# Bucket bits with bits on partitions, and values straight into two padded buffers, in a one-core attention and feed-forward kernel

## The chip, the cores and the metric

The kernel runs on one core of a Trainium2 chip. The metric is the device time of one execution in microseconds (us). Engines are called as in the profile: PE (matrix engine), PEld (its weight loads), DVE (vector), ACT (scalar), POOL (GpSimd) and SP (the queue that issues all DMAs here).

## What is computed

The input x has 16 batches of 512 tokens with 128 features. Each batch goes through hashed attention (16 heads of 8 features) and a feed-forward part; both are layer-normed and added to the residual. What matters for the change is the bucket of each token and head, and the values:

```python
q = (x @ Wq.T + bq).reshape(B, S, H, Dh)
v = (x @ Wv.T + bv).reshape(B, S, H, Dh)
qa = concatenate([q, ones], axis=-1)
proj = einsum('bshe,en->bshn', qa, hyperplanes)          # 6 hyperplanes
bits = (proj >= 0).astype(int32)
buckets = einsum('bshn,n->bsh', bits, 2 ** arange(6))
same = (buckets of s == buckets of t)
attn = softmax(q q^T / sqrt(128) * (62 + same))          # per head
out = attn @ v
```

Afterwards `y1 = x + layernorm(out)`, and the feed-forward part takes the layer-normed y1 through a gated layer of 512 hidden features (Silu), two hidden layers 512 x 512 (Gelu) and an output layer, then the output is `y1 + layernorm(ffn)`.

## The kernel before

One batch is one iteration of `stages` (line 348), and several batches are under way at once: in iteration i the kernel attends to batch i, projects batch i+1 (buckets and values), makes the queries of batch i+2, and runs the feed-forward of batches i-1 and i-2. Iterations -2, -1 and 0 start this up; iterations 2 to 14 carry everything up to the projection, iteration 14 makes no more queries, iteration 15 does not project.

An iteration has 64 slots (`TILES`), one for each score tile of 128 x 512 (16 heads times 4 row tiles). Every engine runs through the same slots in its own program; what it does in a slot is fixed by the constants of lines 55 to 133 (`PROJ_SLOT`, `V_SLOT` and so on), and inside a slot by the order in `iteration`. There is no dynamic order: an engine that waits for a semaphore holds up all that stands behind it. The steady work of a slot is:

- PE: the score tile (line 496) into one of four banks; every fourth slot the row maxima of a head are spread (line 504). The score of tile k waits until DVE has finished tile k-3.
- DVE: the coefficients 62 + same (line 695) for tile k+1, then coefficient times score and its row maximum (line 714); seven heads have one subtraction of the maximum on DVE (line 830).
- ACT copies maxima (line 942); POOL subtracts scores from them (line 899); ACT takes exponentials of two tiles (line 951).
- PE weighs the values with the probabilities, four heads at a time (line 525), in slots 27, 29 and 30 of each quad of heads (`PV_LAGS`), into the one auxiliary bank `aux_bank`. Projections, values, rows and queries use that bank too, in turns.

The steps around the change, by slot, in iterations from 2 on:

- Slot 18: ACT copies the values `v_next` of the batch now attended into `v_pad` (line 1063), where each head has 32 columns: 8 values, a one, zeros.
- Slot 19: PE projects the queries on the hyperplanes, four matmuls of 96 columns (line 568), tokens on partitions; DVE adds the bias in PSUM (line 779).
- Slot 20: DVE compares with zero and multiplies with powers of two (line 785).
- Slot 21: DVE sums the six bits (line 792) into `bcol`, read by the coefficients of the next iteration as a column per head and row tile.
- Slot 21 also holds, on ACT, two Gelus of the second hidden layer (line 1037, `SECOND_GELU_SLOTS` 85 = 64 + 21) and then the normalisation of the attention result (line 956); POOL adds the residual in slot 22 (line 917), DVE takes the statistics of it in slot 23 (line 722).
- Slot 24: PE makes the values (line 557), which wait for the bits since both use `aux_bank`; DVE adds the bias into `v_next` (line 774); ACT casts `bcol` to bf16 (line 994).
- Slot 27: the first weighing (line 525) waits for the value add, `pe.wait_ge(v_next_done, b + 2)` in line 515, since it overwrites that bank.
- Slot 36: PE turns the bucket columns into rows with an identity (line 579), ACT copies them (lines 1002, 1004), SP stores and later broadcasts them.
- Slots 77 to 94, that is 13 to 30 of the next iteration, hold the second hidden layer on PE (line 639), slots 57 to 72 the first (line 629).

At the very start DVE fills `pow2_sb` and clears the stacks, POOL makes an identity and clears `v_pad` (lines 870 to 877), and DVE casts the identity to bf16 (line 837) before its first statistics.

Of the kernel before, what the change touches and what calls it, by code (L numbers as in the profile page):

```python
# [102 lines left out]
V_PAD_SLOT = 18  # L103
# [33 lines left out]
def sandwich_kernel(nc, x, wqT, bq, wvT, bv, hyper_blocks, hyper_bias, w1T, w2T, h1T, h2T, scales, w3T, w3_s, out):  # L137
    ctx = ExitStack()
    with ctx:  # L139
# [19 lines left out]
        hbias_sb = sb("hbias_sb", [P, NH, H])  # L159
        pow2_sb = sb("pow2_sb", [P, NH, H])  # L160
# [8 lines left out]
        ident16 = sb("ident16", [P, P], BF16)  # L169
# [13 lines left out]
        v_next = sb("v_next", [P, ST, H, DH])  # L183
        proj = sb("proj", [P, ST, NH, H])
        bcol16 = sb("bcol16", [P, ST, H], BF16)
# [12 lines left out]
        v_pad = sb("v_pad", [P, ST, H, VW])  # L198
# [48 lines left out]
        v_next_done = sem("v_next_done")  # L247
        proj_psum = sem("proj_psum")
        proj_done = sem("proj_done")
        bits_done = sem("bits_done")  # L250
        bcol_done = sem("bcol_done")
        bcol16_done = sem("bcol16_done")
# [6 lines left out]
        v_pad_done = sem("v_pad_done")  # L259
# [104 lines left out]
        def _(sp):  # L364
            sp.dma_start(x_in[:], x_view[0]).then_inc(x_loaded, 16)
            for dst, src in (
                (wq_sb[:], wqT), (bq_sb[:], bq.rearrange("(p a) -> p a", a=1)),
                (wv_sb[:], wvT), (bv_sb[:], bv.rearrange("(a e) -> a e", a=1).broadcast_to([P, E])),
                (hyper_sb[:], hyper_blocks),
                (hbias_sb[:].rearrange("p n h -> p (n h)"),  # L370
                 hyper_bias.rearrange("(a e) -> a e", a=1).broadcast_to([P, NH * H])),
            ):
                sp.dma_start(dst, src).then_inc(projection_in, 16)
# [93 lines left out]
        def _(pe):  # L467
            pe.wait_ge(projection_in, 16 * PROJECTION_DMAS)
            pe.wait_ge(consts_made, 4)
# [38 lines left out]
            def weigh_values(b, quad, j, query, project):  # L508

                if j == 0:  # L510
                    if quad == 0:
                        pe.wait_ge(v_pad_done, b + 1)

                    if quad == 0 and project:
                        pe.wait_ge(v_next_done, b + 2)
# [8 lines left out]
                for hh in range(4):  # L524
                    last = nc.tensor.matmul(aux_bank[hh * VW:(hh + 1) * VW, :], v_pad[:, j, quad * 4 + hh, :],  # L525
                                            probs[:, quad % 2, hh, j, :], start=(j == 0), stop=(j == ST - 1))
# [25 lines left out]
            def project_step(p, k, attend):  # L552
                if k == V_SLOT:
                    if begun(p):
                        pe.wait_ge(bits_done, p + 1)
                    for t in range(ST):
                        last = nc.tensor.matmul(projection_bank(p, 1)[:, t * P:(t + 1) * P], xnT[:, t * P:(t + 1) * P], wv_sb[:],
                                                start=True, stop=True)
                    last.then_inc(v_psum, 1)
                if k == PROJ_SLOT:  # L560
# [4 lines left out]
                    if begun(p - 1):  # L565
                        pe.wait_ge(att_done, (p - 1) * QUADS)
                    for t in range(ST):
                        last = nc.tensor.matmul(projection_bank(p, 0)[:, t * NH * H:(t + 1) * NH * H], qT[:, t * P:(t + 1) * P],
                                                hyper_sb[:], start=True, stop=True)
                    last.then_inc(proj_psum, 1)  # L570
                if k == ROW_SLOT:
                    pe.wait_ge(consts_made, 5)
                    pe.wait_ge(bcol16_done, p + 1)
# [3 lines left out]
                    for t in range(ST):  # L577

                        last = nc.tensor.matmul(projection_bank(p, 2)[0:H, t * P:(t + 1) * P], bcol16[:, t, :], ident16[:],
                                                start=True, stop=True)  # L580
                    last.then_inc(brow_psum, 1)
# [102 lines left out]
        def _(dve):  # L684
            for n in range(NH):
                last = nc.vector.memset(pow2_sb[:, n, :], float(2 ** n))
            last.then_inc(consts_made, 1)
# [77 lines left out]
            def project_step(p, k):  # L765
                if k == V_ADD_SLOT:
                    dve.wait_ge(v_psum, p + 1)
                    if begun(p):

                        dve.wait_ge(v_pad_done, p)  # L770
                    if isinstance(p, int) and p == 0:

                        dve.wait_ge(projection_in, 16 * PROJECTION_DMAS)
                    nc.vector.tensor_tensor(v_next[:].rearrange("p t h d -> p t (h d)"),
                                            projection_bank(p, 1)[:].rearrange("p (t e) -> p t e", t=ST),
                                            bv_sb[:].unsqueeze(1).broadcast_to([P, ST, E]), ALU.add).then_inc(v_next_done, 1)
                if k == PROJ_ADD_SLOT:
                    dve.wait_ge(proj_psum, p + 1)
                    nc.vector.tensor_tensor(projection_bank(p, 0)[:, 0:ST * NH * H].rearrange("p (t e) -> p t e", t=ST),
                                            projection_bank(p, 0)[:, 0:ST * NH * H].rearrange("p (t e) -> p t e", t=ST),  # L780
                                            hbias_sb[:].rearrange("p n h -> p (n h)").unsqueeze(1).broadcast_to([P, ST, NH * H]),
                                            ALU.add).then_inc(proj_done, 1)
                if k == BITS_SLOT:
                    dve.wait_ge(proj_done, p + 1)
                    nc.vector.scalar_tensor_tensor(out=proj[:].rearrange("p t n h -> p t (n h)"),
                                                   in0=projection_bank(p, 0)[:, 0:ST * NH * H].rearrange("p (t e) -> p t e", t=ST),
                                                   scalar=0.0,
                                                   in1=pow2_sb[:].rearrange("p n h -> p (n h)").unsqueeze(1).broadcast_to([P, ST, NH * H]),
                                                   op0=ALU.is_ge, op1=ALU.mult).then_inc(bits_done, 1)
                if k == BUCKET_SLOT:  # L790
                    dve.wait_ge(bits_done, p + 1)
                    nc.vector.reduce_sum(bcol[:, p % 2], proj[:].rearrange("p t n h -> p t h n"), AXIS_X).then_inc(bcol_done, 1)
# [76 lines left out]
        def _(pool):  # L869
# [4 lines left out]
            nc.gpsimd.memset(v_pad[:, :, :, DH:DH + 1], 1.0).then_inc(v_pad_clear, 1)  # L874
# [3 lines left out]
            pool.wait_ge(consts_made, 4)  # L878
# [55 lines left out]
        def _(act):  # L934

            act.wait_ge(consts_made, 4)
# [103 lines left out]
            def iteration(i, query, project, attend, feed, finish):  # L1040
# [3 lines left out]
                for k in range(TILES):  # L1044
# [12 lines left out]
                    if k == V_PAD_SLOT and attend:  # L1057
                        act.wait_ge(v_next_done, i + 1)

                        if begun(i):  # L1060
                            act.wait_ge(pv_psum, i * QUADS)
# [48 lines left out]
```

## Time and profile before

| | before |
|---|---|
| median of 3 runs | 1501.82 us (1500.60 to 1503.36) |
| profiled execution, its own time | 1501.84 us |
| its span in the profile | 1499.6 us |
| mean granted clock of PE | 0.985 of full |
| instructions | 22142 |

A group's row gives the engine, the operation, what it writes and reads with shapes, how often it ran, its busy time, the mean of one, and the idle time of the engine just before it with what ended it. A timeline row gives the start and the length in us; neighbours of one kind are merged into a row with their count. An idle time in brackets stands in front of the instruction. PE's rows end later than the next one starts, since matmuls are pipelined: how long PE is held is read from start to start. A few matmul records are missing from the trace.

### The profile page before, as it was taken

What the parts mean: (1) busy time and instruction counts of PE and PEld (TensorE: products, weight loads), DVE (VectorE), ACT (ScalarE), POOL (GpSimd) and SP (SyncE); (2) the same over time, 40 slices, a digit from 0 to 9 for tenths busy, and PEclk for the clock granted to TensorE, in tenths of its full rate; (3) what the DMA queues carried; (4) which work ended last, traced back from release to release, by engine and by line L of the source; (5) the groups of instructions that cost most, each with busy time, mean ns of one, the idle gap of its engine ahead of it and who ended that gap; (6) DMA issues with size and microseconds to landing.
All of it is one profiled execution on the core that took longest, in us unless ns stands there. A gap on an engine that the chain in (4) does not pass through costs nothing. (4 is left out here: it accounts for less than half of the span.)

```text
span 1499.6 us, 22142 instructions
## 1 busy us (share of the span) xinstructions
PE 1349.9 (90%) x6502; PEld 625.1 (42%) x6624; DVE 1310.9 (87%) x4026; ACT 1182.8 (79%) x1603; POOL 1216.0 (81%) x809
## 2 busy tenths in 40 slices
PE   3677899999999999999999999899999989999996
PEld 2222344353444435344443534444353444434343
DVE  4999999999999999999999999999999999998620
ACT  2565888888788888878888887888888798888831
POOL 1898979888979988897998889799888979888810
PEclk9888999999999999999999999999999999999999
DMA  5422232222223222222322222232222223212000
GB/s 137 128 55 68 69 85 63 68 68 66 58 68 93 60 71 68 62 62 68 93 58 73 68 60 64 69 93 55 76 69 58 66 68 86 56 50 68 8 1 14
DMA packets 62793, 100.00 MB, mean 67 GB/s; under 512 B 7888, under 2 KB 43984, under 8 KB 62672
## 3 DMA queue, kind: packets, MB, share of 16 engines
q1 hardware_dynamic: 62672, 98.58, 23.6%
q8 instruction: 53, 0.87, 0.3%
q14 instruction: 68, 0.56, 0.1%
HBM read 83.60 MB, written 14.95 MB: 66 GB/s over the span
## 5 line engine op out<-in xcount | busy, mean ns | idle before, releaser
L899 POOL TENSOR_TENSOR logits<-max_row,logits 128x1024 f32<-128x1024 f32 (+1 forms) x512 | 1075.2, 2131 | 133.1 <-ACT max_row L942 130.5
L714 DVE CUSTOM_DVE_ANT_0 logits<-s_bank,coeff 128x512 f32<-128x512 f32 x1024 | 698.4, 683 | 0.6 <-issue 0.6
L695 DVE TENSOR_SCALAR coeff<-brow,bcol 128x516 bf16<-128x516 bf16 x1024 | 483.1, 472 | 79.9 <-PE s_bank L496 37.9
L951 ACT ACTIVATE probs<-logits 128x1024 f32<-128x1024 f32 x512 | 525.5, 1054 | 7.4 <-POOL logits L899 5.1
L496 PE MATMUL s_bank<-mov_stack,stat_stack 128*128 128x512 bf16 x902 | 319.2, 389 | 87.5 <-DVE rowmax L714 43.5
L496 PEld LDWEIGHTS s_bank<-mov_stack,stat_stack 128*128 128x128 bf16 x1024 | 95.2, 98 | 431.2 <-issue 212.0
L525 PE MATMUL aux_bank<-probs,v_pad 128*32 128x512 f32 x2048 | 263.6, 610 | 7.7 <-issue 4.1
L942 ACT COPY max_row<-s_bank 128x512 f32<-128x512 f32 x256 | 148.5, 580 | 137.9 <-PE s_bank L504 136.6
L629 PE MATMUL f_bank<-hid_a,h_sb 128*128 128x512 f32 x512 | 243.1, 596 | 14.9 <-DVE hid_a L809 12.9
L639 PE MATMUL f_bank<-hid_b,h_sb 128*128 128x512 f32 x512 | 249.3, 600 | 1.6 <-ACT hid_b L1032 1.4
L504 PE MATMUL s_bank<-ident,rowmax 128*128 128x128 f32 x1024 | 157.2, 277 | 7.7 <-issue 2.5
L504 PEld LDWEIGHTS s_bank<-ident,rowmax 128*128 128x128 f32 x1024 | 127.4, 139 | 63.9 <-DVE rowmax L714 25.9
L629 PEld LDWEIGHTS f_bank<-hid_a,h_sb 128*128 128x128 f32 x512 | 91.5, 190 | 88.8 <-issue 64.0
L639 PEld LDWEIGHTS f_bank<-hid_b,h_sb 128*128 128x128 f32 x512 | 88.4, 190 | 85.1 <-issue 80.8
L951 ACT ACT_TABLE_LOAD x87 | 111.6, 1283 | 1.5
L525 PEld LDWEIGHTS aux_bank<-probs,v_pad 128*32 128x32 f32 x2048 | 47.8, 109 | 104.0 <-issue 96.9
L714 DVE DVE_READ_ACCUMULATOR2_ANT rowmax<- 128x1 f32 x1024 | 87.3, 85 | 0.0
L830 DVE TENSOR_TENSOR logits<-s_bank,logits 128x512 f32<-128x512 f32 x112 | 77.1, 688 | 3.9 <-ACT max_row L942 3.9
L883 POOL TENSOR_SCALAR end_shift<-end_mv 128x4 f32<-128x4 f32 x16 | 3.1, 193 | 85.3 <-DVE end_mv L727 85.3
L956 ACT ACTIVATE ffn<-ffn,end_bias,end_rstd 128x128 f32<-128x128 f32 x64 | 26.4, 482 | 57.7 <-POOL end_bias L888 57.7
L604 PE MATMUL f_bank<-ynT,w_sb 128*128 128x512 f32 x128 | 66.8, 606 | 1.1 <-ACT ynT L1022 0.7
L618 PE MATMUL f_bank<-ynT,w_sb 128*128 128x512 f32 x128 | 67.0, 606 | 0.3 <-DVE rowmax L714 0.3
(95 smaller groups left out, 1197.1 us busy)
## 6 DMA issues: line engine op xcount, KB each, us to landing
brow<-bucket_scratch SPq DMA_DIRECT2D x64, 522.0 KB
mov_stack<-q_scratch SPq DMA_DIRECT2D x192, 96.0 KB
stat_stack<-q_scratch SPq DMA_DIRECT2D x192, 96.0 KB
q_scratch<-q_parts SPq DMA_DIRECT2D x16, 384.0 KB, 5.4
x_in<-in_x SPq DMA_DIRECT2D x16, 256.0 KB, 7.0
q_scratch<-q_parts SPq DMA_DIRECT2D x16, 256.0 KB, 6.8
x_res<-in_x SPq DMA_DIRECT2D x16, 256.0 KB, 2.9
out<-ffn SPq DMA_DIRECT2D x16, 256.0 KB, 2.6
```

Of the source, the lines that this page charges most:

```text
L496: nc.tensor.matmul(tile_bank(k)[:], stat_stack[:, quad % 2, hh, t * P:(t + 1) * P], mov_stack[:, quad % 2, hh, :], start=True, stop=True). ...
L504: last = nc.tensor.transpose(maxima_bank(h)[:, t * P:(t + 1) * P], rowmax[:, h * ST + t:h * ST + t + 1].broadcast_to([P, P]), ident[:])
L525: last = nc.tensor.matmul(aux_bank[hh * VW:(hh + 1) * VW, :], v_pad[:, j, quad * 4 + hh, :], probs[:, quad % 2, hh, j, :], start=(j == 0), ...
L618: nc.tensor.matmul(f_bank[UP_BANKS[j]][:], w2_sb[:, col], ynT[:], start=True, stop=True).then_inc(w2_psum, 1)
L629: last = nc.tensor.matmul(f_bank[FIRST_HIDDEN_BANKS[j]][:], h1_sb[:, k, col], hid_a[:, k, :], start=(k == 0), stop=(k == HT - 1))
L639: last = nc.tensor.matmul(f_bank[SECOND_HIDDEN_BANKS[j]][:], h2_sb[:, k, col], hid_b[:, k, :], start=(k == 0), stop=(k == HT - 1))
L695: nc.vector.tensor_scalar(coeff[:, k % 3, :].rearrange("p (r n) -> p r n", r=ROW_RUNS), brow[:, h // 4 % 2, h % 4, :, 0:RUN], bcol[:, b % ...
L714: nc.vector.tensor_tensor_reduce(out=logits[:, k % RING, :], in0=tile_bank(k)[:], in1=coeff[:, k % 3, 0:SEQ], scale=float(E) ** -0.5, scal ...
L830: nc.vector.tensor_tensor(logits[:, k % RING, :], maxima_bank(h)[:], logits[:, k % RING, :], ALU.subtract).then_inc(shared_below_max_done, 1)
L899: nc.gpsimd.tensor_tensor(tiles, max_row[:, h % 2, :].unsqueeze(1).broadcast_to([P, n, SEQ]), tiles, ALU.subtract).then_inc(below_max_done, 1)
L942: nc.scalar.copy(max_row[:, h % 2, :], maxima_bank(h)[:]).then_inc(max_row_done, 1)
L951: nc.scalar.activation(probs[:, h // 4 % 2, h % 4, t:t + 2, :], logits[:, k % RING:k % RING + 2, :], ACT.Exp, scale=-1.0).then_inc(probs_d ...
```

## The change

The projection is turned: `hyper_sb` (96 columns) is the stationary operand and all 512 tokens are streamed, so that the 96 bits (6 hyperplanes x 16 heads) lie on partitions. One DVE operation adds the bias, now a column, and compares, and writes bf16 bits. A matrix `weights` with 2^n at (bit n of head h, head h) makes buckets out of bits by matmul: four small ones at slot 21 with the bits stationary give columns, one of 512 columns at slot 36 with the weights stationary gives rows. ACT copies the columns from PSUM to `bcol` in slot 21. The value add moves to slot 25 and writes into one half of a doubled `v_pad`; the copy of slot 18, `v_next`, the bf16 identity and the cast are gone. POOL builds the weights at the start with six selects; DVE casts them before its first statistics. The program is also built with a smaller DMA scratch (8192).

```diff
-V_ADD_SLOT = 24
+V_ADD_SLOT = 25
-PROJ_ADD_SLOT = 19
 BITS_SLOT = 20
-BUCKET_SLOT = 21
-BUCKET_CAST_SLOT = 24
+BCOL_SLOT = 21
+BCOL_COPY_SLOT = 21
-V_PAD_SLOT = 18
...
-        v_pad = sb("v_pad", [P, ST, H, VW])
+        v_pad = sb("v_pad", [P, 2, ST, H, VW])
...
                     if quad == 0:
-                        pe.wait_ge(v_pad_done, b + 1)
+                        pe.wait_ge(v_added, b + 1)
                     if quad == 0 and project:
-                        pe.wait_ge(v_next_done, b + 2)
+                        pe.wait_ge(v_added, b + 2)
...
+                if k == PROJ_SLOT:
...
+                    nc.tensor.matmul(projection_bank(p, 0)[0:NH * H, :], hyper_sb[:], qT[:], start=True,
+                                     stop=True).then_inc(proj_psum, 1)
+                if k == BCOL_SLOT:
+                    pe.wait_ge(weights_made, 1)
+                    pe.wait_ge(bits_done, p + 1)
+                    for t in range(ST):
+                        last = nc.tensor.matmul(projection_bank(p, 0)[:, t * H:(t + 1) * H], bitsT[:, t * P:(t + 1) * P],
+                                                weights16[:], start=True, stop=True)
+                    last.then_inc(bcol_psum, 1)
                 if k == V_SLOT:
                     if begun(p):
-                        pe.wait_ge(bits_done, p + 1)
+                        pe.wait_ge(bcol_done, p + 1)
...
-                        last = nc.tensor.matmul(projection_bank(p, 2)[0:H, t * P:(t + 1) * P], bcol16[:, t, :], ident16[:],
-                                                start=True, stop=True)
-                    last.then_inc(brow_psum, 1)
+                    nc.tensor.matmul(projection_bank(p, 2)[0:H, :], weights16[:], bitsT[:], start=True,
+                                     stop=True).then_inc(brow_psum, 1)
...
                 if k == V_ADD_SLOT:
                     dve.wait_ge(v_psum, p + 1)
...
+                    nc.vector.tensor_tensor(v_pad[:, p % 2, :, :, 0:DH],
+                                            projection_bank(p, 1)[:].rearrange("p (t h d) -> p t h d", t=ST, d=DH),
+                                            bv_sb[:].rearrange("p (h d) -> p h d", d=DH).unsqueeze(1).broadcast_to([P, ST, H, DH]),
+                                            ALU.add).then_inc(v_added, 1)
+                if k == BITS_SLOT:
+                    dve.wait_ge(proj_psum, p + 1)
...
+                    nc.vector.tensor_scalar(bitsT[:], projection_bank(p, 0)[0:NH * H, :], hbias_sb[:], 0.0, ALU.add,
+                                            ALU.is_ge).then_inc(bits_done, 1)
...
-                    dve.wait_ge(consts_made, 4)
-                    nc.vector.tensor_copy(ident16[:], ident[:]).then_inc(consts_made, 1)
+                    dve.wait_ge(weights_built, NH + 1)
+                    nc.vector.tensor_copy(weights16[:], weights_sb[:]).then_inc(weights_made, 1)
...
+            nc.gpsimd.memset(weights_sb[:], 0.0).then_inc(weights_built, 1)
+            for n in range(NH):
+                pool.wait_ge(weights_built, n + 1)
+                nc.gpsimd.affine_select(out=weights_sb[:], in_=weights_sb[:], compare_op=ALU.not_equal,
+                                        fill=float(2 ** n), base=-H * n, pattern=[[-1, H]],
+                                        channel_multiplier=1).then_inc(weights_built, 1)
...
-                if k == BUCKET_CAST_SLOT:
-                    act.wait_ge(bcol_done, p + 1)
-                    nc.scalar.copy(bcol16[:], bcol[:, p % 2]).then_inc(bcol16_done, 1)
+                if k == BCOL_COPY_SLOT:
+                    act.wait_ge(bcol_psum, p + 1)
+                    if p > 1:
+                        act.wait_ge(coeff_done, (p - 1) * TILES)
+                    nc.scalar.copy(bcol[:, p % 2],
+                                   projection_bank(p, 0)[:, 0:ST * H].rearrange("p (t h) -> p t h", t=ST)).then_inc(bcol_done, 1)
...
-                    if k == V_PAD_SLOT and attend:
-                        act.wait_ge(v_next_done, i + 1)
...
-                        nc.scalar.copy(v_pad[:, :, :, 0:DH], v_next[:]).then_inc(v_pad_done, 1)
...
-    nc = bacc.Bacc("TRN2", target_bir_lowering=False, num_devices=1)
+    nc = bacc.Bacc("TRN2", target_bir_lowering=False, num_devices=1, dynamic_dma_scratch_size=8192)
```

## Rows read from the trace of the kernel before

**Rows 1.** The page, part 1: busy time, share of the span, instructions by engine.
```profile
PE 1349.9 (90%) x6502; PEld 625.1 (42%) x6624; DVE 1310.9 (87%) x4026; ACT 1182.8 (79%) x1603; POOL 1216.0 (81%) x809
```

**Rows 2.** Groups by line, whole span: busy us, mean ns | idle before.
```profile
L792 DVE TENSOR_REDUCE bcol<-proj 128x64 f32<-128x384 f32 x16 | 13.0, 814 | 0.0
...
L1063 ACT COPY v_pad<-v_next 128x512 f32<-128x512 f32 x16 | 10.0, 622 | 0.0
...
L779 DVE TENSOR_TENSOR aux_bank<-aux_bank,hbias_sb 128x384 f32<-128x384 f32 x15 | 8.5, 564 | 0.0
L785 DVE SCALAR_TENSOR_TENSOR proj<-aux_bank,pow_sb 128x384 f32<-128x384 f32 x15 | 8.3, 555 | 0.0
...
L994 ACT CAST bcol<-bcol 128x64 bf16<-128x64 f32 x16 | 3.7, 230 | 4.0 <-DVE bcol L792 4.0
```

**Rows 3.** Waits of DVE, 600 to 1290 us (eight iterations): total, times, longest.
```profile
DVE coeff L695 <- PE s_bank L496: 18.6, 32, 1.2
DVE coeff L695 <- remote: 16.1, 8, 2.0
```

**Rows 4.** Timeline, slots 18 to 27: start us, us, engine, line [idle before <-releaser].
```profile
741.35 1.03 PE L568 MATMUL aux_bank<-hyper_sb,qT 128*128 128x96 f32 x8
...
742.21 1.05 PE L639 MATMUL f_bank<-hid_b,h_sb 128*128 128x512 f32 x2
...
743.10 0.38 PE L496 MATMUL s_bank<-mov_stack,stat_stack 128*128 128x512 bf16 x1
...
743.50 1.28 ACT L1037 ACT_TABLE_LOAD   x1
743.51 0.48 DVE L695 TENSOR_SCALAR coeff<-brow,bcol 128x516 bf16<-128x516 bf16 x1
...
744.52 0.56 DVE L785 SCALAR_TENSOR_TENSOR proj<-aux_bank,pow_sb 128x384 f32<-128x384 f32 x1
...
745.03 0.38 PE L496 MATMUL s_bank<-mov_stack,stat_stack 128*128 128x512 bf16 x1
...
745.23 1.27 ACT L1037 ACTIVATE hid_a<-f_bank,scales_sb 128x512 f32<-128x512 f32 x2 [0.45 <-PE f_bank L639]
...
745.45 0.48 DVE L695 TENSOR_SCALAR coeff<-brow,bcol 128x516 bf16<-128x516 bf16 x1 [0.37 <-PE s_bank L496]
...
748.11 1.27 POOL L917 TENSOR_TENSOR y<-y,x_res 128x512 f32<-128x512 f32 x1 [0.34 <-ACT y L956]
...
749.41 0.88 DVE L722 BATCH_NORM_STATS2 att_stats<-y 128x6 f32<-128x128 f32 x4
...
751.19 0.69 DVE L774 TENSOR_TENSOR v_next<-aux_bank,bv_sb 128x512 f32<-128x512 f32 x1
...
753.56 1.92 PE L525 MATMUL aux_bank<-probs,v_pad 128*32 128x512 f32 x16
```

**Rows 5.** Timeline, six iterations later, slot 21.
```profile
1271.00 0.48 DVE L695 TENSOR_SCALAR coeff<-brow,bcol 128x516 bf16<-128x516 bf16 x1 [0.38 <-PE s_bank L496]
```

**Rows 6.** Timeline, the end of slot 30 and slot 31.
```profile
758.70 1.98 PE L639 MATMUL f_bank<-hid_b,h_sb 128*128 128x512 f32 x4
...
760.94 0.48 DVE L695 TENSOR_SCALAR coeff<-brow,bcol 128x516 bf16<-128x516 bf16 x1 [2.01 <-remote]
```

**Rows 7.** Timeline of ACT, slot 52.
```profile
785.66 0.59 ACT L976 COPY xnT<-aux_bank 128x512 f32<-128x512 f32 x1 [0.41 <-PE aux_bank L546]
786.26 1.28 ACT L1027 ACT_TABLE_LOAD   x1
```

**Rows 8.** Timeline, the first 21 us.
```profile
0.90 1.80 POOL L872 MEMSET v_pad<- 128x2048 f32 x1
...
5.57 0.85 DVE L722 BATCH_NORM_STATS2 x_stats<-x_in 128x6 f32<-128x128 f32 x4
...
17.19 1.97 PE L557 MATMUL f_bank<-wv_sb,xnT 128*128 128x128 f32 x8
...
20.35 0.58 PE L579 MATMUL f_bank<-ident,bcol 128*16 128x128 bf16 x4 [1.19 <-ACT bcol L994]
```

More of the change, by code:

```diff
@@ L524, in weigh_values @@
                 for hh in range(4):
-                    last = nc.tensor.matmul(aux_bank[hh * VW:(hh + 1) * VW, :], v_pad[:, j, quad * 4 + hh, :],
+                    last = nc.tensor.matmul(aux_bank[hh * VW:(hh + 1) * VW, :], v_pad[:, b % 2, j, quad * 4 + hh, :],
                                             probs[:, quad % 2, hh, j, :], start=(j == 0), stop=(j == ST - 1))
@@ L552, in project_step @@
             def project_step(p, k, attend):
-                if k == V_SLOT:
-                    if begun(p):
-                        pe.wait_ge(bits_done, p + 1)
-                    for t in range(ST):
-                        last = nc.tensor.matmul(projection_bank(p, 1)[:, t * P:(t + 1) * P], xnT[:, t * P:(t + 1) * P], wv_sb[:],
-                                                start=True, stop=True)
-                    last.then_inc(v_psum, 1)
                 if k == PROJ_SLOT:
@@ L566, in project_step @@
                         pe.wait_ge(att_done, (p - 1) * QUADS)
-                    for t in range(ST):
-                        last = nc.tensor.matmul(projection_bank(p, 0)[:, t * NH * H:(t + 1) * NH * H], qT[:, t * P:(t + 1) * P],
-                                                hyper_sb[:], start=True, stop=True)
-                    last.then_inc(proj_psum, 1)
+                    nc.tensor.matmul(projection_bank(p, 0)[0:NH * H, :], hyper_sb[:], qT[:], start=True,
[3 more added lines that the diff above has]
+                    pe.wait_ge(bits_done, p + 1)
+                    for t in range(ST):
+                        last = nc.tensor.matmul(projection_bank(p, 0)[:, t * H:(t + 1) * H], bitsT[:, t * P:(t + 1) * P],
+                                                weights16[:], start=True, stop=True)
+                    last.then_inc(bcol_psum, 1)
+                if k == V_SLOT:
+                    if begun(p):
+                        pe.wait_ge(bcol_done, p + 1)
+                    for t in range(ST):
+                        last = nc.tensor.matmul(projection_bank(p, 1)[:, t * P:(t + 1) * P], xnT[:, t * P:(t + 1) * P], wv_sb[:],
+                                                start=True, stop=True)
+                    last.then_inc(v_psum, 1)
                 if k == ROW_SLOT:
-                    pe.wait_ge(consts_made, 5)
-                    pe.wait_ge(bcol16_done, p + 1)
                     if attend:
                         pe.wait_ge(att_done, (p - 1) * QUADS + 1)
-                    for t in range(ST):
-                        last = nc.tensor.matmul(projection_bank(p, 2)[0:H, t * P:(t + 1) * P], bcol16[:, t, :], ident16[:],
-                                                start=True, stop=True)
-                    last.then_inc(brow_psum, 1)
+                    nc.tensor.matmul(projection_bank(p, 2)[0:H, :], weights16[:], bitsT[:], start=True,
+                                     stop=True).then_inc(brow_psum, 1)
             def ffn_step(f, slot, finish):
@@ L684, in _ @@
         def _(dve):
-            for n in range(NH):
-                last = nc.vector.memset(pow2_sb[:, n, :], float(2 ** n))
-            last.then_inc(consts_made, 1)
             nc.vector.memset(brow16[:], 0.0).then_inc(stacks_clear, 1)
@@ L767, in project_step @@
                     dve.wait_ge(v_psum, p + 1)
-                    if begun(p):
[L770 to L789, printed above, removed]
@@ L873, in _ @@
             pool.wait_ge(v_pad_clear, 1)
-            nc.gpsimd.memset(v_pad[:, :, :, DH:DH + 1], 1.0).then_inc(v_pad_clear, 1)
+            nc.gpsimd.memset(v_pad[:, :, :, :, DH:DH + 1], 1.0).then_inc(v_pad_clear, 1)
             pool.wait_ge(consts_made, 1)
```

39 lines of the change are left out of this document (18 added, 21 removed).

## The prediction

> **What bounds the kernel now.** I read the page first, then the groups by line, the waits, and the timeline of one iteration engine by engine. The page calls PE and DVE the two busiest engines [rows 1]; an average cannot say which of them a saving must come from, and the change takes work from DVE above all. The timeline can: the same event of two iterations six apart stands at 745.45 and 1271.00 us [rows 4, 5], so one iteration takes 525.55 / 6 = 87.59 us, and its pattern repeats to a hundredth. One iteration has 64 slots, a score tile each (about 1.0 us on DVE). In slots 0 to 31 PE also carries the hidden layers of the feed-forward: between 730 and 761 us no matmul row shows idle time in front of it, and it is DVE that waits. In eight iterations DVE waited 18.6 us for score matmuls and 16.1 us for "remote" [rows 3]. The second is PE too: DVE stands 2.01 us before slot 31's tile, until 760.94 [rows 6], just as PE is through with the four instructions that began at 758.70; that tile's matmul record is missing. So each iteration has 2.0 us of DVE waiting at slot 31, and the edited steps (slots 18 to 25) all lie in front of it. After slot 31 the roles change, but nothing of weight is edited there.
>
> **What the change removes from DVE.** Three operations of 0.564, 0.555 and 0.814 us [rows 2] go. By starts in the timeline they hold DVE 0.47, 0.47 and 0.73 us, 1.67 together. The new bits operation (96 x 512 out of PSUM) is not in the trace. Its lower bound is the 384-element comparison, 0.555; its upper one the 512-element add, 0.69 [rows 4]. The length is 512, so 0.69, which holds DVE 0.60. Net 1.07 us an iteration. None of it reaches the end in a full iteration: tile 20 starts at 743.51 because its score matmul began at 743.10 and took 0.38, and tile 21 at 745.45 for the one that began at 745.03 [rows 4]. The add before tile 20 becomes a wait, the comparison is replaced at its place, and the saved reduction comes before tile 22, where PE is next late and from where slot 31's wait swallows the rest.
>
> **What it does on PE.** The four projections (eight instructions from 741.35 until the next line starts at 742.21, 0.86 us) become one pair of 512 columns; the pair of that size at 742.21 is over when the score matmul starts at 743.10, 0.89 [rows 4]. Zero. The buckets' four small matmuls at slot 21 are new. Eight load-and-multiply steps of the projection take 0.86, 0.107 each, so four take 0.43; below, 0.1 (their 16 columns alone), above, 0.6 (loads not hidden). I take 0.43 by the nearest row. The row matmul at slot 36 gets shorter by at most 0.2 where PE waits for DVE: zero.
>
> **What it moves on ACT.** The 0.622 us copy into the padded buffer goes and the 0.230 us cast too [rows 2]; ACT has idle time there: zero. But the new copy of the bucket columns stands at slot 21 and waits for the new matmuls, and queued behind it on ACT are the load of the Gelu table, two Gelus, and the normalisation whose result DVE needs at slot 23. Now the table load runs at 743.50, before the Gelus are due, and they start at 745.23 when PE is ready [rows 4]. With the copy in front the load should come later: at slot 52 a copy that waits for PE stands ahead of a Silu, and the load began at 786.26, after the copy of 785.66 to 786.25 [rows 7]. Step by step: bits start at 744.52 (where the comparison starts now) and end at 745.21; the matmuls run from 745.26, and the last result is there at about 745.78; ACT sees it at 745.84; a copy of 0.23 ends at 746.07; the load of 1.28 ends at 747.36. The Gelus start at 747.37, 2.14 late. Normalisation and the residual on POOL (748.11 now) follow without slack, for DVE waits for them already: its statistics start at 749.41, 0.03 after POOL is done [rows 4]. They move to 751.55.
>
> **Who waits for that.** The value add moves from slot 24 to 25. After the statistics come tile 24 (start to start 1.78 with them), the moments 0.28, tile 25 0.99 and the add 0.69: it ends at 755.29. PE's value matmuls of slot 27 wait for this add because both use the auxiliary bank. They start at 753.56 now [rows 4], with 1.7 us in hand since the add started at 751.19. They would start at 755.34, 1.78 late. The four bucket matmuls' 0.43 lies inside that. PE has no idle time from there to slot 31, so that tile and the iteration are 1.78 us later. In the half after it DVE, PE, ACT and POOL are shifted alike; POOL's lost 2.1 us go into its idle time.
> This holds for the 13 iterations that carry projection, Gelu at slot 21 and residual together (2 to 14): 13 x 1.78 = 23.1 us.
>
> The load is 1.28 us in the trace, and the next activation starts right after it (743.50 to 744.78; the Gelus then wait for PE) [rows 4]. The Trainium skill, page "ScalarE: Activation LUTs", section "What ACT_TABLE_LOAD costs", gives 1283 ns for the load and about 1380 ns more for a drain, 2.66 us for each switch. By that the Gelus would start 1.38 us later still, and the 13 iterations would cost 18 us more.
>
> **First iterations and start.** In iterations 0 and 1 PE is light and DVE sets the pace; between 0 and 2 x 1.07 us are won, I take 1.1, since PE must now answer between slots 20 and 22. At the start POOL's clearing of the padded buffer doubles, 1.80 us more [rows 8], with the identity behind it. Then a small memset and six dependent selects of small size, not in the trace; POOL's small dependent steps are 0.27 apart, so 1.6 (bounds 0.1 and 0.4 each: 0.6 and 2.4). They are ready at about 6.9, DVE copies them, and the first statistics start at 7.1 instead of 5.57 [rows 8]: 1.5. Before the first bucket row PE now does the columns and the value product (1.97 [rows 8]) behind the bits: bits end at 18.64, columns 19.3, values 21.2, row 21.85, against 20.93 now (20.35 + 0.58): 0.9. The DMA issues follow the row. Start: 2.4 us, bounds 0.5 to 4.
>
> **Sum.** 23.1 + 2.4 - 1.1 = 24.4. The profiled execution took 1501.84 us (span 1499.6), the median is 1501.82, so no correction: 1526 us, 1.6% slower. A difference under 0.2% (3 us) is what a measurement of this kernel cannot tell from none.
>
> **Rivals.**
> A. The table load runs ahead of the copy, or the copy finds its data earlier. For: the load itself needs nothing of the copy. Against: rows 7. Then the Gelus start at 746.08, 0.85 late, the value add ends at 754.0 and PE is only 0.4 to 0.5 later an iteration: 13 x 0.45 + 1.3 = 7 us, 1509.
> B. Faster, because DVE's saving counts in full: the mechanism is that PE is not the last to arrive in slots 19 to 31, for example if it runs ahead as soon as DVE reads its banks sooner. Price 15 x 1.07 = 16.1, less 2.4 at the start: 1488. For: DVE's busy share [rows 1]. Against: the 2.01 us of waiting behind all the edits [rows 6]. It decides only where that wait would be under 1.07.
> C. Slower still, by the switch of 2.66 us, or with PE's later matmuls also running into DVE's shared subtraction at slot 27: 1544. Against: the trace's load has no such tail.
> D. As A, but with bucket matmuls of 0.1 and Gelus that PE keeps waiting anyway: 13 x 0.1 + 1.3 = 2.6 us, 1504, within what can be told from none.
>
> **Chances.** Forecast 0.62, A 0.18, B 0.08, C 0.07, D 0.05. The forecast's own range: the delay of 2.14 may be 0.4 smaller or larger (bucket matmuls 0.1 to 0.6, copy from PSUM 0.2 to 0.3), 13 x 0.4 = 5, and the start 2: 1519 to 1532. To hold the time 8 times in 10 the range reaches down through A: 1506 to 1532. Slower 0.62 + 0.18 + 0.07 = 0.87, same 0.05, faster 0.08.
>
> **What would show it.** Right: the period is about 89.4 us; the Gelu table load of slot 21 starts after the bucket copy, near 2.6 us later against slot 20 than now; DVE waits about 2 us for the residual before the statistics of slot 23; the value matmuls of slot 27 have about 1.4 us idle before them, released by the value add; slot 31's wait is still between 1.5 and 2 us. Wrong: a period under 88.1 (then A, or a smaller delay), a load that begins before the copy, a wait at slot 31 that is gone together with a period under 87 (B). If DVE shows no wait for the residual at slot 23, the step that fails is the one on ACT's queue.

## The result, and the profile after

The changed kernel takes 1526.23 us (median of 4 runs, 1524.69 to 1527.95) against 1501.59 us for the kernel before on the same chip: ratio 1.0163, 95% interval 1.0145 to 1.0181, so slower by 24.6 us. The forecast was 1526.0. The span of the profiled execution is 1524.2 us against 1499.6.

The page, part 1, of the changed kernel:

```profile
PE 1360.0 (89%) x6429; PEld 615.2 (40%) x6544; DVE 1296.2 (85%) x3988; ACT 1174.3 (77%) x1587; POOL 1218.9 (80%) x816
```

DVE's busy time fell by 14.7 us against [rows 1] and the span grew by 24.6: the saving is there and worth nothing. The new operations, groups by line (busy us, mean ns | idle before, and what ended it):

```profile
L776 DVE TENSOR_SCALAR bitsT<-aux_bank,hbias_sb 96x512 bf16<-96x512 f32 x15 | 11.1, 742 | 0.0
...
L767 DVE TENSOR_TENSOR v_pad<-aux_bank,bv_sb 128x512 f32<-128x512 f32 x15 | 10.3, 686 | 0.0
...
L988 ACT COPY bcol<-aux_bank 128x64 f32<-128x64 f32 x15 | 3.2, 212 | 40.6 <-PE aux_bank L561 40.6
```

ACT stood 40.6 us in front of fifteen copies of 0.212 us; the cast it replaces had 4.0 us in front of sixteen [rows 2]. The waits of DVE from 600 to 1310 us, eight iterations (total, times, longest):

```profile
DVE coeff L687 <- PE s_bank L491: 26.5, 48, 1.9
DVE att_stats L714 <- POOL y L908: 15.3, 8, 1.9
DVE coeff L687 <- remote: 13.7, 15, 1.9
```

The second line is new: eight waits of 1.9 us for the residual, absent from [rows 3]. The timeline of one iteration, slots 21 to 27 and 31 (a time here less 13.28 us compares with [rows 4, 6]: the comparison began at 744.52, the bits begin at 757.80):

```profile
757.80 0.74 DVE L776 TENSOR_SCALAR bitsT<-aux_bank,hbias_sb 96x512 bf16<-96x512 f32 x1
...
758.31 0.38 PE L491 MATMUL s_bank<-mov_stack,stat_stack 128*128 128x512 bf16 x1
...
758.68 0.24 PE L561 MATMUL aux_bank<-weights,bitsT 96*128 96x16 bf16 x4
...
758.78 1.11 PE L634 MATMUL f_bank<-hid_b,h_sb 128*128 128x512 f32 x2
...
758.97 0.21 ACT L988 COPY bcol<-aux_bank 128x64 f32<-128x64 f32 x1 [2.70 <-PE aux_bank L561]
...
759.20 1.28 ACT L1032 ACT_TABLE_LOAD   x1
...
760.49 1.26 ACT L1032 ACTIVATE hid_a<-f_bank,scales_sb 128x512 f32<-128x512 f32 x2
...
763.36 1.27 POOL L908 TENSOR_TENSOR y<-y,x_res 128x512 f32<-128x512 f32 x1 [2.32 <-ACT y L947]
...
764.67 0.87 DVE L714 BATCH_NORM_STATS2 att_stats<-y 128x6 f32<-128x128 f32 x4 [1.92 <-POOL y L908]
...
767.71 0.69 DVE L767 TENSOR_TENSOR v_pad<-aux_bank,bv_sb 128x512 f32<-128x512 f32 x1
...
768.46 0.19 PEld L520 LDWEIGHTS aux_bank<-probs,v_pad 128*32 128x32 f32 x8 [1.79 <-DVE v_pad L767]
...
768.49 1.92 PE L520 MATMUL aux_bank<-probs,v_pad 128*32 128x512 f32 x16 [1.24 <-ACT probs L942]
...
775.87 0.48 DVE L687 TENSOR_SCALAR coeff<-brow,bcol 128x516 bf16<-128x516 bf16 x1 [1.89 <-remote]
```

Read from the top: ACT is idle for 2.70 us at a copy of 64 columns, the table load starts only behind it, the Gelus come 1.98 us later than before (760.49 - 13.28 = 747.21 against 745.23), the residual and with it the statistics again 1.98 (751.39 against 749.41), the value add ends at 768.40, and the value matmuls of slot 27 start at 755.21 against 753.56: 1.65 late. Six iterations later the bits begin at

```profile
1293.08 0.74 DVE L776 TENSOR_SCALAR bitsT<-aux_bank,hbias_sb 96x512 bf16<-96x512 f32 x1
```

so the period is (1293.08 - 757.80) / 6 = 89.21 us against 87.59: 1.62 more, over 13 iterations 21.1 of the 24.6 us. The start, from the same timeline at its beginning, answers to [rows 8]:

```profile
0.90 3.51 POOL L857 MEMSET v_pad<- 128x4096 f32 x1
...
5.35 1.89 POOL L867 TENSOR_SCALAR_AFFINE_SELECT weights_sb<-weights_sb 96x16 f32<-96x16 f32 x6
...
7.35 0.86 DVE L714 BATCH_NORM_STATS2 x_stats<-x_in 128x6 f32<-128x128 f32 x4
...
22.63 0.60 PE L575 MATMUL f_bank<-bitsT,weights 96*16 96x512 bf16 x1
```

Where each tile comes late shows where the iteration loses (start of the tile's logits within an iteration, against the same tile before):

```
tile      19    22    23    24    26    28    31 to the end
after      0  -0.35 +0.17 +1.94 +1.94 +1.75  +1.62
```

Two steps need explaining: +1.9 at the statistics, and that 1.62 of it is never made good.

### The profile page after: what moved, and what is told of

Read it like the earlier page. It is cut to its first block and busy times, and to the rows that moved or that the text cites. A ratio compares the mean times of both kernels' runs of the same rounds, so it can differ in the third digit from the quotient of the medians.

```text
span 1524.2 us, 21959 instructions
## 1 busy us (share of the span) xinstructions
PE 1360.0 (89%) x6429; PEld 615.2 (40%) x6544; DVE 1296.2 (85%) x3988; ACT 1174.3 (77%) x1587; POOL 1218.9 (80%) x816
## 5 line engine op out<-in xcount | busy, mean ns | idle before, releaser
L491 PE MATMUL s_bank<-mov_stack,stat_stack 128*128 128x512 bf16 x909 | 324.1, 391 | 75.6 <-DVE rowmax L706 34.1
```

The costliest lines, as they stand in the source:

```text
L491: nc.tensor.matmul(tile_bank(k)[:], stat_stack[:, quad % 2, hh, t * P:(t + 1) * P], mov_stack[:, quad % 2, hh, :], start=True, stop=True). ...
```

## The experiments

Eleven kernels ran. The theory (T): the bucket copy on ACT, queued before the table load, delays the residual; the value add is queued on DVE behind the residual's statistics; PE waits for the add, and PE has no idle time to make that good before slot 31. The rivals: the delay comes from more work on PE; the wait in slot 27 is for ACT's exponentials, as the PE row above names it; or the doubled buffer and the direct value path cost the time.

**1. The copy off ACT's queue.** The same copy on DVE, in its slot; all else is the change.

```
 on DVE, slot 21:
+  dve.wait_ge(bcol_psum, p + 1)
+  nc.vector.tensor_copy(bcol[:, p % 2], projection_bank(p, 0)[:, 0:ST * H]...)
 on ACT, slot 21:
-  act.wait_ge(bcol_psum, p + 1)
-  nc.scalar.copy(bcol[:, p % 2], projection_bank(p, 0)[:, 0:ST * H]...)
```

> The changed kernel with one step moved: the bucket columns are copied out of PSUM by DVE in slot 21 instead of by ACT. Theory (the copy on ACT's queue holds back the Gelu table load, and through the residual and the value add PE's slot 27): the Gelus start when PE is ready, the value add ends before PE wants it, and the period falls from 89.21 to 87.59 + 0.10 (the four bucket matmuls, 0.10 as measured) = 87.7 us. Total about 1501.6 + 2.4 (start) + 1.3 + 0 to 2 for iterations 0 and 1: 1505 to 1508. Rival 1 (the bucket matmuls and the turned projection on PE are the cost): the period stays at 89.2, 1526. Rival 2 (writing values with a stride of 32, or the doubled buffer, slows the work): period stays above 88.5.

Measured: 1511.96 us (4 runs, 1510.20 to 1512.79), ratio to before 1.0066 (1.0049 to 1.0083), period 88.07: 1.14 of the 1.62 us are gone, and 14.3 us of the 24.6, though the same copy is still made. Waits of DVE, eight iterations:

```profile
DVE coeff L687 <- PE s_bank L491: 28.9, 53, 1.9
DVE coeff L687 <- remote: 18.4, 20, 1.9
```

The waits for the residual have left the list. So most of the loss is the copy's place in ACT's queue; but the total missed the expected 1505 to 1508, and what is left over lies in two places. In slot 27 PE still waits for the add:

```profile
672.36 0.69 DVE L767 TENSOR_TENSOR v_pad<-aux_bank,bv_sb 128x512 f32<-128x512 f32 x1
...
673.12 0.19 PEld L520 LDWEIGHTS aux_bank<-probs,v_pad 128*32 128x32 f32 x8 [0.78 <-DVE v_pad L767]
```

and in slot 21 the small matmuls cost PE 0.31 us (there the next score matmul starts 4.39 us after tile 19, 4.09 before). Both were tried next.

**2. The add one slot earlier,** ahead of the statistics' tile, where it was before; the copy stays on ACT.

```
-V_ADD_SLOT = 25
+V_ADD_SLOT = 24
```

> The changed kernel with the value add back in slot 24. The trace names the exponentials as what PE's value matmuls of slot 27 wait for (10.0 us in eight iterations); the theory says it is the value add, which ends 0.05 us before them too. Theory: with the add one tile earlier PE is next held by the shared subtraction of slot 27, which is 1.98 us late with 1.2 in hand: the period is 87.59 + 0.85 = 88.4 us, and iteration 1 no longer loses 2.5 us. Rival (the exponentials hold PE): the period stays at 89.2.

Measured: 1513.78 us (2 runs, 1513.5 to 1514.06), ratio 1.0080 (1.006 to 1.010), period 88.46. DVE still stands before the statistics, as in the change,

```profile
DVE att_stats L714 <- POOL y L908: 15.4, 8, 1.9
```

so the residual is as late as in the change, and yet 0.75 us an iteration come back. That names what PE waited for in slot 27: the add. The exponentials stood where they were (the one that ends as PE starts in the change begins 12.1 us after tile 19's logits in both kernels), while PE's value matmuls of slot 27 came from 13.16 to 11.90, ahead of it; so the PE row names the exponentials wrongly and the weight-load row above it (1.79 <-DVE v_pad) names the add rightly. Iteration 1 went from 85.10 to 81.51 us, which matters below.

The 0.87 us a period that are left are more than the value matmuls are late now (11.90 against 11.53, 0.37). The late residual reaches PE by a second road, as the expectation said: DVE is late with its tiles and with the shared subtraction of slot 27, and two score matmuls wait for it.

```profile
673.67 0.39 PE L491 MATMUL s_bank<-mov_stack,stat_stack 128*128 128x512 bf16 x1 [0.29 <-DVE rowmax L706]
...
675.37 0.38 PE L491 MATMUL s_bank<-mov_stack,stat_stack 128*128 128x512 bf16 x1 [0.31 <-DVE logits L815]
```

**3. The value path alone,** on the kernel before: the add writes into the doubled padded buffer, the ACT copy goes, everything of the buckets stays.

```
-v_pad = sb("v_pad", [P, ST, H, VW])
+v_pad = sb("v_pad", [P, 2, ST, H, VW])
-nc.vector.tensor_tensor(v_next[:]..., projection_bank(p, 1)..., bv_sb..., ALU.add)
+nc.vector.tensor_tensor(v_pad[:, p % 2, :, :, 0:DH], projection_bank(p, 1)..., bv_sb..., ALU.add)
-nc.scalar.copy(v_pad[:, :, :, 0:DH], v_next[:])
```

(The DMA scratch is cut to 8192 bytes, as in the change.)

> The kernel before with one part of the change alone: values are added straight into two padded buffers in slot 24 and the ACT copy of slot 18 is gone; projection, bits and buckets as before. Theory: the period stays at 87.59 us (ACT has idle time there) and only the longer clearing of the buffer shows at the start, if the identity is late for DVE's cast: at most 1.8 us, total 1501.6 to 1503.4. Rival: the freed 0.62 us of ACT is worth something, period under 87.4, or the strided add is slower and the period is above 87.8.

Measured: 1501.61 us (8 runs), ratio 1.0002 (0.9991 to 1.0012), period 87.59, to a hundredth that of before. The 0.622 us copy taken off ACT [rows 2] is worth nothing, and the direct path costs nothing. The period's whole loss belongs to the buckets and the slot of the add.

**4. The copy stays on ACT, one slot later,** behind the table load and the Gelus.

```
-BCOL_COPY_SLOT = 21
+BCOL_COPY_SLOT = 22
```

> The changed kernel with the copy still on ACT but in slot 22, behind the table load, the Gelus, the normalisation and the copy of the maxima. Theory: the residual chain is on time again, but PE's value matmuls of slot 24 wait for the copy, which ends 0.6 us after PE gets there: the period is 88.0 to 88.3 us. Rival (ACT's copy as such costs, wherever it stands): the period stays near 89.2.

Measured: 1515.35 us (2 runs), ratio 1.0091 (1.007 to 1.0111), period 88.44, a little above the 88.0 to 88.3 expected; the rival's 89.2 is out. No wait for the residual is left here either. So it was the place in ACT's queue, not the copy's being on ACT. The 0.37 above the copy on DVE is the link that the expectation named: PE's value matmuls of slot 24 need the bank of the columns and wait for the copy.

```profile
669.97 0.97 PEld L568 LDWEIGHTS aux_bank<-wv_sb,xnT 128*128 128x128 f32 x8 [0.59 <-ACT bcol L988]
```

The hidden-layer matmuls behind them start 0.36 us later than in experiment 1 (7.59 against 7.23 us after tile 19's logits).

**5. Experiments 1 and 2 together.**

> The changed kernel with the bucket columns copied by DVE in slot 21 and the value add in slot 24. With the copy alone moved the period was 88.07 us, 0.48 over before: PE was 0.31 late after the bucket matmuls, and its slot 27 stood 0.16 more for the value add in slot 25. Theory: with both edits only PE's 0.31 is left, period 87.9 us, and iterations 0 and 1 gain about 1 us each instead of losing; with 2.3 us at the start the total is about 1505.5. Rival: the value add's place is worth nothing here, period 88.07.

Measured: 1506.51 us (7 runs), ratio 1.0034 (1.0021 to 1.0046), period 87.90. Taking the copy away saved 1.14 and moving the add 0.75; both together save 1.31, not 1.89, since they shorten one chain.

**6. The bucket matmuls a slot later too,** so that PE need not wait for the bits.

```
-BCOL_SLOT = 21
-BCOL_COPY_SLOT = 21
+BCOL_SLOT = 22
+BCOL_COPY_SLOT = 22
```

(on top of 5)

> As the run before it (copy on DVE, add in slot 24), with the four bucket matmuls and their copy one slot later, in slot 22. Theory: of PE's 0.31 us, 0.13 to 0.17 is its wait for the bits in slot 21; in slot 22 the bits are long done, and the period is 87.75 us. Rival: all of the 0.31 is the matmuls and the weight loads around them, which are not hidden, and the period stays at 87.9.

Measured: 1504.13 us (8 runs), ratio 1.0022 (1.0011 to 1.0034), period 87.74. The best placing found for the change's own steps, with all of DVE's saving in it, is still 0.15 us a period above the kernel before.

**7. Is slot 31 really PE's?** [Rows 3, 6] put DVE's wait there down to "remote", and the prediction to PE. On the kernel before, the last two of PE's second-layer groups move past slot 31:

```
-SECOND_HIDDEN_SLOTS = (..., 88, 88, 88, 90, 94, 94)
+SECOND_HIDDEN_SLOTS = (..., 88, 88, 88, 90, 95, 96)
```

> The kernel before, with two matmuls of the second hidden layer moved from slot 30 to slots 31 and 32 (two constants, 94, 94 to 95, 96), same work. Theory (PE bounds the slots up to 31, DVE those behind it, and DVE's 2.01 us wait at slot 31 is the seam): tile 31 comes 1.72 us earlier, the wait falls to 0.3, and PE does the two matmuls where it has idle time: period 85.9 us, 14 iterations, 1501.6 - 24 = 1478. Rival (the wait at slot 31, which the trace puts down to a remote releaser, is a DMA or something else than PE): nothing changes, 1501.6; or the matmuls are missed behind slot 31, and the gain is under 0.9 an iteration.

Measured: 1492.88 us (3 runs), ratio 0.9949 (0.9926 to 0.9971), period 86.94. The "remote" wait of 2.0 us is gone: it was PE. But only 0.65 us of the expected 1.7 stayed, as in the last of the rivals (a gain under 0.9): tile 31 came 1.81 us sooner, tile 35 gave back 1.17. Slot 34 holds three output matmul groups, and they wait for the second pair of Gelus:

```profile
672.27 2.94 PE L648 MATMUL f_bank<-w_sb,hid_a 128*128 128x128 f32 x24 [0.68 <-ACT hid_a L1037]
```

The Gelus stand where they stood in the kernel before (19.67 us after tile 19's logits in both), so the output matmuls start only 0.42 us sooner than there (20.98 against 21.40), not 1.8. Behind slot 31 ACT is thus one more bound.

**8. The mechanism alone, on the kernel before.** There the cast of the bucket columns stands in slot 24, behind the Gelus. One constant puts it ahead of the table load:

```
-BUCKET_CAST_SLOT = 24
+BUCKET_CAST_SLOT = 21
```

> The kernel before with one constant changed: ACT's cast of the bucket columns in slot 21 instead of 24. It waits there for DVE's reduction (ends about 3.7 us after tile 20's coefficients begin) and stands ahead of the Gelu table load, as the new copy does in the changed kernel. Theory (a copy that waits ahead of the load pushes load, Gelus, normalisation and residual back one for one): the Gelus start about 3.5 us late, DVE waits 3.4 us for the residual, PE's slot 27 and its score of slot 30 come 1.9 to 2.4 late: period 89.5 to 90.0, total 1526 to 1533, with no other part of the change in it. Rival (the load is not held up, or the chain has slack): period within 0.2 of 87.59.

Measured: 1535.69 us (2 runs), ratio 1.0228 (1.0198 to 1.0258), period 90.12. This is the strongest evidence: no arithmetic is added or taken away, only a 0.25 us cast moved up in ACT's queue, and the kernel loses 34 us, a little more than expected (89.5 to 90.0, 1526 to 1533). Its timeline:

```profile
673.35 0.25 ACT L994 CAST bcol<-bcol 128x64 bf16<-128x64 f32 x1 [3.81 <-DVE bcol L792]
...
673.61 1.28 ACT L1037 ACT_TABLE_LOAD   x1
...
674.91 1.26 ACT L1037 ACTIVATE hid_a<-f_bank,scales_sb 128x512 f32<-128x512 f32 x2
...
677.78 1.26 POOL L917 TENSOR_TENSOR y<-y,x_res 128x512 f32<-128x512 f32 x1 [3.98 <-ACT y L956]
...
679.07 0.87 DVE L722 BATCH_NORM_STATS2 att_stats<-y 128x6 f32<-128x128 f32 x4 [3.76 <-POOL y L917]
...
680.99 0.39 PE L496 MATMUL s_bank<-mov_stack,stat_stack 128*128 128x512 bf16 x1 [1.08 <-DVE rowmax L714]
681.64 1.92 PE L525 MATMUL aux_bank<-probs,v_pad 128*32 128x512 f32 x16 [0.26 <-DVE v_next L774]
```

Up to the statistics it is the same chain as in the change with larger numbers: ACT waits 3.81 us at the cast, DVE 3.76 us before the statistics; 2.53 us of it are in the period. The last link differs. Here the add is in slot 24 and PE waits only 0.26 us for it; it is held 1.08 us just before, at a score matmul that waits for DVE's late tile. So the experiment shows that the place in ACT's queue costs the time; that the add passes it on in the change is shown by experiment 2.

**9. The start.** On top of 6, POOL makes the identity and the weights first and clears the padded buffer last, so that the statistics need not wait for the clearing.

```
-nc.gpsimd.memset(v_pad[:], 0.0)      # ahead of the identity and the weights
+nc.gpsimd.memset(v_pad[:], 0.0)      # behind them
```

> Copy on DVE and bucket matmuls in slot 22, add in slot 24 (period 87.74), with POOL's start in another order: identity and weights first, the clearing of the padded buffers behind them. Theory: DVE's first statistics start at about 5.7 us instead of 7.35, the start costs 1.6 us less, and the total is 1502 to 1503: the change without its misplaced steps is worth nothing and costs nothing in a kernel whose slots 0 to 31 are bound by PE. Rival: the clearing now delays POOL's first rstd (it ends near 7.1, just when the statistics are there) and nothing is won, 1504.

Measured: 1504.08 us (10 runs), ratio 1.0015 (1.0005 to 1.0024). The first row's second copy came 1.06 us earlier than in 6 (22.62 against 23.68), not 1.6 or more, and the time did not move. The timeline shows why the start gained less:

```profile
3.60 3.51 POOL L873 MEMSET v_pad<- 128x4096 f32 x1
...
5.32 1.82 DVE L828 CAST weights<-weights_sb 96x16 bf16<-96x16 f32 x1
5.33 1.80 DVE L714 BATCH_NORM_STATS2 x_stats<-x_in 128x6 f32<-128x128 f32 x4
```

The cast of 16 columns, 0.17 us in the changed kernel, takes 1.82 and ends at 7.14, with POOL's clearing at 7.11; the statistics queue behind it. The program no longer makes DVE wait for the clearing, but DVE's cast now takes as long as the clearing does. Why the 1.06 us that were won do not show in the total either is not shown; the first tile's logits start at 34.24 us here and at 34.31 in 6, so they are lost by then.

**10 and 11. The search for a version that beats both.** If PE in slots 19 to 31 is the bound, its work should be spread. Both kernels got the same three edits, 10 on top of 9 (all of the change), 11 on the kernel before:

```
-SECOND_HIDDEN_SLOTS = (..., 90, 94, 94)      OUTPUT_SLOTS = (98, 98, 98, 99)     FFN_SLOT = 35
+SECOND_HIDDEN_SLOTS = (..., 90, 95, 96)      OUTPUT_SLOTS = (98, 99, 99, 100)    FFN_SLOT = 37
```

> The kernel of the run before, with PE's work spread: the two second-hidden matmuls of slot 30 in slots 31 and 32, output matmuls in slots 34, 35, 35, 36 instead of 34, 34, 34, 35, and DVE's scaling of them in slot 37 instead of 35. With the first of these alone tile 31 came 1.81 us sooner and tile 35 gave 1.17 back, since three output matmuls stand in slot 34. Theory: with the spread most of it is kept; period 86.0 to 86.6, total 1478 to 1487, faster than both kernels. Rival: PE's later slots have no room, the loss only moves to slots 36 to 41, period about 87, 1492.

> The kernel before with the same three edits of PE's and DVE's slots. It is the control for the run before it: if DVE's saving by the change (1.0 us an iteration in slots 19 to 21) is worth anything once PE's seam at slot 31 is smaller, this kernel is slower than that one by up to 0.7 us an iteration (9 us); if PE still bounds slots 0 to 31, it is faster by 0.15 us an iteration (the bucket matmuls), 2 us. I expect the second: period 85.8 to 86.5.

Measured: with the change 1493.22 us (4 runs), ratio 0.9943 (0.9929 to 0.9958), period 87.00; without it 1491.81 us (4 runs), ratio 0.9932 (0.9915 to 0.9950), period 86.86. Both beat both kernels; the gain is all of the three constants. The two intervals overlap, so their totals do not rank them, but the periods differ by 0.14 as expected: even now DVE's saving is not worth anything. The target of 86.0 to 86.6 was missed. Spread output groups only moved the give-back to tiles 36 to 39 (tile 35 is 1.8 us sooner, the iteration 0.73). The waits of DVE in 11:

```profile
DVE coeff L695 <- PE s_bank L496: 23.6, 49, 1.2
...
DVE coeff L695 <- remote: 4.3, 8, 0.5
```

Against [rows 3] 11.8 us of "remote" went and 5.0 of PE came. PE's output matmuls still wait 5.4 us in eight iterations for the Gelus, in 10 as in 11, and not at all in the kernel before, so the give-back is in part ACT's; no experiment moved the Gelus.

## Why the prediction was right

**Mechanism.** Right at every link of the steady iteration. The load starts behind the copy; experiments 1 and 4 (copy taken from the head of the queue) and 8 (a cast put there) show that the queue is the cause, 2 shows the add as the second link, 7 that slot 31's wait is PE's. The signs that it named are there: the table load is 2.42 us later (2.6 said), DVE waits 1.92 us at the statistics (2), PE's row 1.24 in slot 27 (1.4), and 1.89 us are left at slot 31 (1.5 to 2). What it did not see is the second road of experiments 2 and 8: with the add in slot 24 there would still be 0.87 us a period. The links of the steady iteration, each against its measured value:

```
term                                     predicted   measured
bits op on DVE                             0.69        0.742
four bucket matmuls, start to next start   0.43        0.10
Gelus late                                 2.14        1.98
statistics late                            2.14        1.98
value matmuls of slot 27 late              1.78        1.65
period longer                              1.78        1.62
13 iterations                             23.1        21.1
iterations 0 and 1                        -1.1        +2.56 (0.07 and 2.49)
start, at the first row's second copy     +2.4        +2.29
start, at the first tile's logits         +2.4        +1.03
```

**The bucket matmuls, mis-sized.** They were priced like the projection's steps of 128 x 96 in f32; the 16-column bf16 ones go at 0.025 each (758.68 to 758.78), the lower bound named. But PE also waits 0.17 for the bits, so the whole PE cost at slot 21 was 0.31, measured in experiment 1. On the chain they make the copy begin 1.17 us after the bits (757.80 to 758.97), where 1.32 was predicted: that is 0.15 of the 0.16 between 2.14 and 1.98.

**What the prediction said of PE's 0.43 lying inside the delay** holds: in the change no more than 1.62 of 1.98 reach the period, and the slot-21 cost only shows once the chain is shortened (experiments 5 and 6: 0.16 an iteration).

**The projection at zero, the ACT copies at zero** hold (3: no difference; tile 19 and all before it unchanged). **DVE's saving at zero** holds in every version: -0.35 us at tile 22, nothing at tile 31.

**The table load.** The load starts at 759.20 and the first Gelu at 760.49, 1.29 us later, although here, unlike before, nothing else holds the Gelu. The copy in front of the load ends at 759.18, so there is no room before it either; and in [rows 4] the load ended 0.45 us before the Gelus. So the trace shows no 1.38 us drain at this load: the figure of the Trainium skill ("ScalarE: Activation LUTs", "What ACT_TABLE_LOAD costs", 2.66 us a switch) would have put the result near 1544, and does not hold here. Rival C falls with it.

**The step that failed: "In iterations 0 and 1 [...] between 0 and 2 x 1.07 us are won, I take 1.1".** Iteration 1 took 85.10 us against 82.61, 2.5 longer. From slot 22 to 27 it does run 0.3 to 0.8 us ahead, as said; tile 28 is 1.5 late. Iteration 1 has a residual and a value add too, and PE is so light that it is early at slot 27's matmuls and waits there for the add. The waits of PE in that iteration include

```profile
PE aux_bank L520 <- DVE v_pad L767: 1.3, 1, 1.3
```

and with the add back in slot 24 the iteration takes 81.51 us (experiment 2), 1.1 under the kernel before: a gain is real there and was buried by the slot of the add.

The loss is more than that wait, for PE's matmuls behind it also ran at a lower clock. These are the value matmuls of slot 27 in iteration 1, in the kernel before and in the changed one, and the latter's row of a view by windows (the last three numbers are PE's granted clock, the DMA share and GB/s):

```profile
142.69 1.92 PE L525 MATMUL aux_bank<-probs,v_pad 128*32 128x512 f32 x16 [0.26 <-issue]
...
144.78 3.64 PE L520 MATMUL aux_bank<-probs,v_pad 128*32 128x512 f32 x16 [1.31 <-DVE v_pad L767]
...
145.00:147.00 2.00, 2.00 (x12) 0.45 (x8) 2.00 (x7) 1.06 (x1) 1.75 (x4) 0.50 0.00 0
```

The granted clock was 0.50 from 143 to 149 us, the lower of its two levels (1.2 of 2.4 GHz); in the kernel before it was 1.00 during these matmuls. From 141 to 143 us, where it fell, PE was busy for 0.13 us: it stood 2.09 us for DVE, ran one score tile, then stood 1.31 for the add. The matmuls start 0.80 us later against tile 19's logits (10.31 against 9.51) and take 1.72 longer: together the 2.5. In experiments 2 and 5 they take 1.92 again at 1.00, and between 1 and 5, which differ by the add's slot alone, iteration 1 goes from 83.66 to 81.49 us. But the fall came before the wait for the add, and what part of the low stretch is due to the add was not separated: in experiment 8, with the add in slot 24 and a wait of 1.55 us for DVE before them, they took 2.88, and iteration 1 took 84.67 us.

The total came out within 0.3 us because the errors cancel: against their terms the steady iterations came out 2.0 under, the first two 3.7 over, the start 1.4 under by the first tile's logits. A forecast this near is partly luck; the 1.62 against 1.78 is its real precision.

## What to carry to other kernels

Each engine here took its work in the order of its program (experiment 8): before a small copy is put on an engine, look at what is queued behind it, and ask how long the copy waits, not how long it runs. Here 0.21 us of copying delayed a table load by 2.4 us, and the delay passed from ACT to POOL, DVE and PE before it became time. Work taken from an engine is worth nothing while that engine waits for another one behind the edit; find that last wait first, for moving three constants around it was worth 10 us here, and 15 us of removed DVE work none.

## What the runs showed of the hardware

- A cast of 16 columns on DVE beside POOL's memset of 4096 columns took 1.82 us instead of 0.17 and ended 0.03 us after the memset (experiment 9); DVE's own memset (1.76 us, starting at 3.62) ran beside it at its usual length (1.76 also when it is the first, at 1.48). The Trainium skill, page "SBUF — State Buffer", section "SBUF: two separate sides", says that GpSimd and a DVE operation in some modes share one pair of ports, which the one that starts first keeps for its whole instruction while the other is blocked; the cast's row agrees.
- Sixteen value matmuls took 1.92 us at a granted clock of 1.00 and 3.64 us at 0.50 (iteration 1 of the kernel before and of the changed one, above).
- A releaser named in a row can be wrong where several semaphores are waited for: the PE row of slot 27 names the exponentials, the weight-load row the add, and experiment 2 decides for the add. "remote" stood for matmuls whose records are missing (experiment 7).
- At the start the first tile's logits began anywhere between 31.3 and 35.2 us over the thirteen kernels, whose row copy stood within 2.3 us, and over 2.6 us for those whose row copy stood within 0.03. DVE's first coefficients wait for the DMA that brings the bucket rows: its landing varies, so that a start term of 1 to 2 us is to be read at the row copy, not from a total.
